# Two output matmuls at a time: regrouping the second layer's blocks in a slot of TensorE's order

## Chip, cores and metric

One NeuronCore of a Trainium2 chip runs the whole program. The metric is the device time of one execution in microseconds (us); lower is better. TensorE (PE in the profile) does matmuls and transposes into PSUM, VectorE (DVE), ScalarE (ACT) and GpSimd (POOL) do elementwise work, and SyncE (SP) issues nearly all DMA transfers.

## What is computed

The input is x, 32 images of 128 channels by 56 by 56 pixels, in float32. Cut to what matters:

```
z = x + relu(batchnorm(conv3x3(sign(ln_channels(x)), sign(w) * alpha) + b))
t = tokens(z)                         # 32 x 3136 tokens x 128 channels
u = layernorm(t)
weights = u @ wr + br                 # one number a token
sel = the 1567 tokens of an image with the largest weights
f[sel] = (gelu(u[sel] @ w1 + b1) @ w2 + b2) * weights[sel];  f = 0 elsewhere
out = from_tokens(t + f + u)
```

w1 is 128 x 512 and w2 512 x 128. The kernel computes the two layers for all tokens and multiplies with a gate that is 0 for the tokens not chosen.

## The kernel before

**Tiling.** Channels lie on the 128 partitions. An image is 3136 columns, worked in 7 chunks of 448 (`NCH = 7`, `T = 448`). Everything below names a chunk by its number c, 0 to 6.

**Two phases.** Phase 1 (up to about 565 us) does the convolution of all images and sums up the batch statistics. Phase 2 does the rest, and the change lies in it alone. It is a software pipeline over images: while image n is in its two layers, image n+1 is normalised, image n+2 gets its residual, and the outcome of image n-1 is gated and stored.

**Positions.** Phase 2 gives each image 56 positions (`POS = 2 * NB * NCH`), in 7 slots of 8. Each engine walks through the same positions, in an order written out by hand, and does at each what tables name for it. `due(table, shift, n, b, pos)` says which steps fall on this position; an entry of 56 or more falls into the next image's positions. In slot c of image n TensorE does:

- positions 0 to 3 of the slot: `hidden`, the four blocks of the first layer of chunk c (three fp16 matmuls each, L939 to L941);
- positions 4 to 7: `output`, the four blocks of the second layer of chunk c-1, accumulated in one PSUM bank (one float32 matmul each; the profile shows each as two MATMUL records of L950). In slot 0 it is the last chunk of the image before. The last block raises `y_done`, and ScalarE copies the bank out (L505) at the eighth position.

**Steps between them.** Behind the hidden or output block of a position TensorE does what the tables place there. In this text each has a short name with its chunk or round:

- T0 to T6 (`TRANSPOSE_AT`, L885): four transposes of a chunk of image n+1 for its layernorm. VectorE takes statistics of each (L647). T2 waits until the statistics of T0 are taken, T3 for those of T1, since they share PSUM banks.
- N0 to N6 (`NORM_AT`, L917 and L920): the statistics as rows of 3 partitions spread to 128 partitions by two matmuls. VectorE scales and centres with them (L685, then L694 one position later), and later forms the base of the output (L702).
- R0 to R6 (`ROUTER_AT`, L895): router weights. After R6 they go through DRAM for the search of the threshold.
- C0 to C7 (`COUNT_AT`, L959): one round each of that search. VectorE counts (L722), TensorE sums the counts (C), VectorE chooses and sets the next candidates (L728, L733, L739) and counts again for the next round.
- G0 to G6 (`OUT_AT`, L930): the gates of image n-1 spread from 3 partitions to 128. VectorE multiplies with them (L781), GpSimd adds the base.
- ST (L904), the mask step (L965 to L967) and the scan (L972), once an image.

The steps that fall on the fifth to eighth position of each slot, behind the output block there, are:

| slot | fifth | sixth | seventh | eighth |
|---|---|---|---|---|
| 0 | T2 | T3, C7 | | N4 |
| 1 | | scan | | R0, N5 |
| 2 | R3, N6 | R4 | | R5, ST |
| 3 | | G2 | | N0 |
| 4 | | | G4 | C1, N1 |
| 5 | | G5 | C3 | N2 |
| 6 | G6 | C5 | N3 | |

VectorE's own order at a position is: choose (L728), first count or gates, tile statistics (L647), L685, L733, L694, L781, L739, L702, next count (L722). L694 of chunk 3 falls on the last position of the image and is VectorE's last instruction there.

**The loop.** `pairs` writes images -1 to 2 and 29 to 32 out straight, and runs images 3 to 28 in a loop on each engine, two images a turn: 13 turns, 12 jumps back to the loop's start (ahead of images 5, 7, ... 27). The loop's own instructions have line L269.

Of the kernel before, what the change touches and what calls it, by code (L numbers as in the profile page):

```python
# [21 lines left out]
NCH = TOK // T  # L22
# [6 lines left out]
NB = HID // C  # L29
# [48 lines left out]
def block_kernel(nc, consts, x_in, cw_in, cb_in, gamma_in, beta_in, wr_in, br_in, w1_in, b1_in,  # L78
# [12 lines left out]
    with ExitStack() as ctx:  # L91
# [167 lines left out]
        def wait_count(eng, semaphore, value):  # L259

            if not (isinstance(value, int) and value <= 0):
                eng.wait_ge(semaphore, value)
# [12 lines left out]
        def is_int(n):  # L275
            return isinstance(n, int)

        def has(n, low=0, high=n_img):

            return not is_int(n) or low <= n < high  # L280
# [6 lines left out]
        def due(table, shift, n, b, pos):  # L287

            steps = [table] if is_int(table) else table
            found = []  # L290
            for at, m, mb in ((pos, n + shift, (b + shift) % 2), (pos + POS, n + shift - 1, (b + shift + 1) % 2)):
                if at in steps and has(m):
                    found.append((m, mb, steps.index(at)))
            return found
# [533 lines left out]
        def _(pe):  # L828
# [46 lines left out]
            def transposes(m, b, c, n, pos):  # L875
                pe.wait_ge(x1_ready, m * NCH + c + 1)

                wait_count(pe, t_ready if c % 2 else u_ready, done(NORM_AT, 1, n, pos))
                if c % 2:
                    wait_count(pe, gated, done(OUT_AT, -1, n, pos))  # L880
                if c > 1:
                    pe.wait_ge(stats_taken, m * NCH + c - 1)
                for i in range(TPG):
                    lo = c * T + i * TILE
                    last = nc.tensor.transpose(ps[0:TILE, BC0 + c % 2, i * C:(i + 1) * C], xb[b][:, lo:lo + TILE], ident)  # L885
                last.then_inc(transposed, 1)

            def router(n, b, c):

                pe.wait_ge(tl_ready, n * NCH + c + 1)  # L890
                if c == 0 and has(n - 1):
                    pe.wait_ge(mask_step, (n - 1) * MASK_STEPS + 3)
                bank = ps[:, T_BANK, 0:T]
                for i, (w, t) in enumerate(((wsel_h, th), (wsel_h, tl), (wsel_l, th))):
                    last = M(bank, w[:, C - c:2 * C - c], cut(t, c), start=c == 0 and i == 0,  # L895
                             stop=c == NCH - 1 and i == 2)
                if c == NCH - 1:
                    last.then_inc(w_done, 1)

            def rows_of_stats(m, n, pos):  # L900
                pe.wait_ge(mr_ready, m + 1)
                wait_count(pe, u_ready, done(NORM_AT, 1, n, pos))
                for q in range(2):
                    last = nc.tensor.transpose(ps[0:NT, BC0, q * C:q * C + TILE], rm[:, q, :],  # L904
                                               ident[0:TILE, 0:TILE])
                last.then_inc(stat_rows, 1)

            def spread_stats(m, b, c, n, pos):

                g = m * NCH + c  # L910
                if c == 0:
                    pe.wait_ge(norm_rows_in, (m + 1) * 2 * PIECES * 16)

                wait_count(pe, u_ready, g)
                wait_count(pe, stats_taken, done(TRANSPOSE_AT, 1, n, pos + 1))
                wait_count(pe, rms_ready, done(STAT_AT, 1, n, pos + 1))
                M(ps[:, BC0, 0:T], ones_b[0:PIECES, :], cut(rows[0:PIECES, :], c), start=True, stop=True).then_inc(bc_stats, 1)  # L917
                wait_count(pe, t_ready, g)
                wait_count(pe, gated, done(OUT_AT, -1, n, pos + 1))
                M(ps[:, BC1, 0:T], ones_b[32:32 + PIECES, :], cut(rows[32:32 + PIECES, :], c), start=True, stop=True).then_inc(bc_stats, 1)  # L920

            def spread_gates(m, b, c, n, pos):
                g = m * NCH + c
                if c == 0:
                    pe.wait_ge(gate_rows_in, (m + 1) * PIECES * 16)

                wait_count(pe, gated, g)
                wait_count(pe, t_ready, done(NORM_AT, 1, n, pos))
                wait_count(pe, stats_taken, done(TRANSPOSE_AT, 1, n, pos + 1))
                M(ps[:, BC1, 0:T], ones_b[64:64 + PIECES, :], cut(rows[64:64 + PIECES, :], c), start=True, stop=True).then_inc(bc_gate, 1)  # L930

            def hidden(n, b, c, j):
                g = n * NCH + c
                if j == 0:
                    pe.wait_ge(tl_ready, g + 1)
                wait_count(pe, h_ready, (g - 1) * NB + j + 1)
                bank = ps[:, H_BANK + j, 0:T]
                blk = slice(j * C, (j + 1) * C)
                M(bank, w1_h[:, blk], cut(th, c), start=True, stop=False)  # L939
                M(bank, w1_h[:, blk], cut(tl, c), start=False, stop=False)  # L940
                M(bank, w1_l[:, blk], cut(th, c), start=False, stop=True).then_inc(h_done, 1)  # L941

            def output(n, b, c, j):
                g = n * NCH + c
                if j == 0:
                    wait_count(pe, y_taken, g)
                first, final = j == 0, j == NB - 1
                bank = ps[:, Y_BANK, 0:T]
                pe.wait_ge(h_ready, g * NB + j + 1)
                last = M(bank, w2_c[:, j, :], hs[(b + c) % 2][:, j, :], start=first, stop=final)  # L950
                if j == NB - 1:
                    last.then_inc(y_done, 1)

            def sum_counts(n, r):

                pe.wait_ge(part_counts, n * ROUNDS + r + 1)
                if r == 0:
                    pe.wait_ge(w_taken, n + 1)
                M(cnt_ps, cnt_c[:, :].to_broadcast([C, C]), cand_sel[:, :], start=True,  # L959
                  stop=True).then_inc(counts_summed, 1)  # L960

            def transpose_ties(n):
                pe.wait_ge(ties_ready, n + 1)
                R = slice(0, MR_ROWS)
                nc.tensor.transpose(ps[0:MR_COLS, T_BANK, 0:MR_ROWS], ties_sb, ident[R, R])  # L965
                M(off_ps, kt[R, K_ONES:K_ONES + MR_ROWS], rowg_c[R, :], start=True, stop=False)
                M(off_ps, kt[R, K_STRI:K_STRI + MR_ROWS], rowe_c[R, :], start=False, stop=True).then_inc(ties_t, 1)  # L967

            def scan_ties(n):

                pe.wait_ge(ties_copied, n + 1)
                M(ps[0:MR_ROWS, T_BANK, C:C + MR_COLS], et[:, :], kt[0:MR_COLS, K_TRIU:K_TRIU + MR_COLS],  # L972
                  start=True, stop=True).then_inc(ties_scanned, 1)

            def phase2(n, b):
                for pos in range(POS):
                    c, j = divmod(pos, 2 * NB)

                    if j < NB and has(n):
                        hidden(n, b, c, j)  # L980
                    if j >= NB and c > 0 and has(n):
                        output(n, b, c - 1, j - NB)
                    if j >= NB and c == 0 and has(n - 1):
                        output(n - 1, 1 - b, NCH - 1, j - NB)

                    at = (n, b, pos)
                    for m, mb, c in due(TRANSPOSE_AT, 1, *at):
                        transposes(m, mb, c, n, pos)
                    for m, mb, c in due(ROUTER_AT, 0, *at):
                        router(m, mb, c)  # L990
                    for m, mb, r in due(COUNT_AT, 0, *at):
                        sum_counts(m, r)
                    for m, mb, _ in due(MASK_AT, 0, *at):
                        transpose_ties(m)
                    for m, mb, _ in due(SCAN_AT, 0, *at):
                        scan_ties(m)
                    for m, mb, _ in due(STAT_AT, 1, *at):
                        rows_of_stats(m, n, pos)
                    for m, mb, c in due(OUT_AT, -1, *at):
                        spread_gates(m, mb, c, n, pos)  # L1000
                    for m, mb, c in due(NORM_AT, 1, *at):
                        spread_stats(m, mb, c, n, pos)

            pairs(pe, phase2, *P2, -1, n_img + 1)


# [20 lines left out]
```

## Time and profile before

| | |
|---|---|
| median of 3 runs | 2377.53 us (2375.41 to 2380.52) |
| time of the profiled execution | 2379.78 us |
| its span, first to last instruction | 2377.8 us |
| busy: PE, DVE, ACT, POOL | 93%, 68%, 51%, 39% |
| mean granted TensorE clock | 0.981 of full |

The profiled execution's own time lies 2.0 us over its span, and 2.3 us over the median of the runs. Busy time is a share of the span; matmuls are pipelined and overlap each other, so that the distance from start to start says more than the time of one. The timeline merges instructions of one line that follow each other ("x4" is four records) and gives the idle time of the engine ahead of an instruction in brackets, with what ended it.

### The profile page before, as it was taken

Reading aid. Unit: us, or ns where it says so; the run is one execution under the profiler, and the core shown is the slowest. Engines: PE = TensorE matmul, PEld = TensorE weight load, DVE = VectorE, ACT = ScalarE, POOL = GpSimd, SP = SyncE. Lnnn points to the kernel's source line nnn. Section 1 sums busy time; section 2 is a strip of 40 time slices with the busy share of each in tenths; the row PEclk is TensorE's granted clock in tenths of the full one; section 3 lists DMA queues with packets and bytes.
Section 4 is the critical chain, followed back from the end, with each engine's and each line's share of the span. In section 5 each row is a group of like instructions: output and inputs, shape, how many; then the busy total and the mean of one; then the engine's idle time right before and its main releaser. Section 6 shows DMA issues by size and latency. Waiting matters only on the chain. (4 is left out here: it accounts for less than half of the span.)

```text
span 2377.8 us, 38759 instructions
## 1 busy us (share of the span) xinstructions
PE 2202.0 (93%) x9739; PEld 1071.6 (45%) x9739; DVE 1622.5 (68%) x4887; ACT 1222.9 (51%) x2030; POOL 918.5 (39%) x714
## 2 busy tenths in 40 slices
PE   6999999966999999999999999998999999999997
PEld 3555555533444444444444444444444444444443
DVE  6777777755677766767676666666667676767764
ACT  4444444434555555555555555555555555555553
POOL 1000000024455544445445555454544454554433
PEclk9999999987999999999999999999999999999998
DMA  3444444431122222222222222222222222222201
GB/s 146 163 162 162 162 162 162 162 122 46 62 73 73 74 81 76 81 85 75 73 73 73 73 73 72 73 73 73 81 82 91 73 73 73 73 73 84 73 33 59
DMA packets 66710, 216.99 MB, mean 91 GB/s; under 512 B 28496, under 2 KB 33328, under 8 KB 62640
## 3 DMA queue, kind: packets, MB, share of 16 engines
q1 hardware_dynamic: 66464, 215.71, 25.1%
q14 instruction: 84, 0.69, 0.1%
q8 instruction: 18, 0.29, 0.1%
q10 hardware_dynamic: 144, 0.30, 0.0%
HBM read 136.70 MB, written 77.47 MB: 90 GB/s over the span
## 5 line engine op out<-in xcount | busy, mean ns | idle before, releaser
L950 PE MATMUL ps<-hs,w_c 128*128 128x448 f32 x1792 | 806.9, 564 | 0.8 <-ACT yo L505 0.6
L495 ACT ACTIVATE hs<-ps,b1c,undo 128x448 f32<-128x448 f32 x896 | 602.6, 718 | 136.6 <-PE ps L941 136.0
L412 POOL TENSOR_TENSOR tl<-tr,th 128x448 f16<-128x448 f32 x224 | 245.5, 1096 | 515.7 <-ACT th L518 393.9
L854 PE MATMUL ps<-yo,cwT 128*128 128x448 bf16 x2016 | 425.6, 356 | 0.0
L950 PEld LDWEIGHTS ps<-hs,w_c 128*128 128x128 f32 x1792 | 305.3, 192 | 191.7 <-issue 152.3
L505 ACT ACTIVATE yo<-ps,cols 128x448 f32<-128x448 f32 x224 | 141.9, 633 | 453.6 <-PE ps L950 453.6
L407 POOL TENSOR_TENSOR xb<-xb,zr 128x448 f32<-128x448 f32 x224 | 259.1, 1159 | 182.7 <-ACT zr L511 181.8
L419 POOL TENSOR_TENSOR yo<-yo,base 128x448 f32<-128x448 f32 x224 | 264.5, 1181 | 167.4 <-DVE yo L781 166.6
L939 PE MATMUL ps<-th,w_h 128*128 128x448 f16 x896 | 321.4, 359 | 0.0
L941 PE MATMUL ps<-th,w_l 128*128 128x448 f16 x896 | 319.3, 356 | 0.0
L940 PE MATMUL ps<-tl,w_h 128*128 128x448 f16 x896 | 319.2, 356 | 0.0
L854 PEld LDWEIGHTS ps<-yo,cwT 128*128 128x128 bf16 x2016 | 179.2, 98 | 196.2 <-issue 48.7
L476 ACT ACTIVATE y<-ps 128x448 f16<-128x448 f32 x224 | 121.9, 544 | 263.2 <-PE ps L854 263.2
L781 DVE TENSOR_TENSOR yo<-yo,ps 128x448 f32<-128x448 f32 x224 | 138.6, 619 | 152.4 <-PE ps L930 150.7
L647 DVE BATCH_NORM_STATS2 st<-ps 112x6 f32<-112x128 f32 x896 | 192.7, 282 | 62.9 <-PE ps L885 60.5
L511 ACT ACTIVATE zr<-y,bn_t,bn_s 128x448 f32<-128x448 f16 x224 | 168.8, 754 | 122.2 <-DMA y<-y_int 109.6
L685 DVE TENSOR_TENSOR ur<-xb,ps 128x448 f32<-128x448 f32 x224 | 138.5, 618 | 134.8 <-PE ps L917 76.5
L571 DVE BATCH_NORM_STATS2 base<-y 128x448 f16 (+1 forms) x224 | 140.5, 627 | 130.2 <-ACT y L476 130.2
L518 ACT ACTIVATE th<-tr 128x448 f16<-128x448 f32 x224 | 129.3, 577 | 139.8 <-DVE tr L694 127.6
L426 POOL TENSOR_TENSOR rm<-stw,kt 112x28 f32<-112x28 f32 x32 | 153.6, 4799 | 78.8 <-DVE stw L665 78.8
L885 PE MATMUL ps<-kt,xb 128*112 128x128 f32 x896 | 140.4, 281 | 41.7 <-DVE st L647 28.8
L403 POOL TENSOR_TENSOR sm<-sm,kt 128x1 f32<-128x1 f32 x1 | 0.6, 566 | 459.7 <-DVE sm L635 459.7
(131 smaller groups left out, 2709.7 us busy)
## 6 DMA issues: line engine op xcount, KB each, us to landing
xb<-x SPq DMA_DIRECT2D x31, 1568.0 KB, 7.6
xb<-x SPq DMA_DIRECT2D x33, 896.0 KB, 4.7
result<-yo SPq DMA_DIRECT2D x32, 896.0 KB, 4.4
y_int<-y SPq DMA_DIRECT2D x32, 784.0 KB, 3.7
xb<-x SPq DMA_DIRECT2D x33, 672.0 KB, 4.3
result<-yo SPq DMA_DIRECT2D x32, 672.0 KB, 3.4
y<-y_int SPq DMA_DIRECT2D x32, 448.0 KB, 5.3
y<-y_int SPq DMA_DIRECT2D x32, 336.0 KB, 4.8
```

The source lines that it names most:

```text
L407: nc.gpsimd.tensor_tensor(cut(xb[b], c), cut(xb[b], c), zr[(b + c) % 2][:, :], ALU.add).then_inc(x1_ready, 1)
L412: nc.gpsimd.tensor_tensor(cut(tl, c), tr[(b + c) % 2][:, :], cut(th, c), ALU.subtract).then_inc(tl_ready, 1)
L419: nc.gpsimd.tensor_tensor(cut(yo[b], c), cut(yo[b], c), cut(base[b], c), ALU.add).then_inc(out_ready, 1)
L426: nc.gpsimd.tensor_tensor(rm[:, 0, :], stw[:, 5, :], kt[0:TILE, K_MHALF:K_END], ALU.pow).then_inc(rstd_ready, 1)
L495: nc.scalar.activation(hs[(b + slot) % 2][:, j, :], ps[:, H_BANK + j, 0:T], ACT.Gelu_apprx_tanh, bias=b1c[:, j:j + 1], scale=undo[:, 1:2]) ...
L511: nc.scalar.activation(zr[(mb + c) % 2][:, :], cut(y16[mb], c), ACT.Relu, bias=bn_t[:, :], scale=bn_s[:, :]).then_inc(relu_ready, 1)
L647: last = V.bn_stats(st[:, c * TPG + i, :], ps[0:TILE, BC0 + c % 2, i * C:(i + 1) * C])
L854: last = M(bank, cwT[:, t, :], sg[b][:, c * ROWS + dy:c * ROWS + dy + ROWS, dx:dx + SIDE], start=t == 0, stop=t == TAPS - 1)
L939: M(bank, w1_h[:, blk], cut(th, c), start=True, stop=False)
L940: M(bank, w1_h[:, blk], cut(tl, c), start=False, stop=False)
L941: M(bank, w1_l[:, blk], cut(th, c), start=False, stop=True).then_inc(h_done, 1)
L950: last = M(bank, w2_c[:, j, :], hs[(b + c) % 2][:, j, :], start=first, stop=final)
```

## The change

The four output blocks of a chunk no longer take one position each. Blocks 0 and 1 are issued at the fifth position of a slot and blocks 2 and 3 at the seventh; the sixth and the eighth issue none. All other steps keep their position and stay behind the output blocks of it. The same instructions are issued, in another order, and only on TensorE.

```diff
                     if j < NB and has(n):
                         hidden(n, b, c, j)
-                    if j >= NB and c > 0 and has(n):
-                        output(n, b, c - 1, j - NB)
-                    if j >= NB and c == 0 and has(n - 1):
-                        output(n - 1, 1 - b, NCH - 1, j - NB)
+                    for k in range(j - NB, j - NB + 2) if j in (NB, NB + 2) else ():
+                        if c > 0 and has(n):
+                            output(n, b, c - 1, k)
+                        if c == 0 and has(n - 1):
+                            output(n - 1, 1 - b, NCH - 1, k)
```

## Rows read from the trace of the kernel before

**Rows 1.** Waits of PE, longest first: in total, times, longest.

```profile
PE ps L917 <- DMA rows<-rms: 43.1, 32, 7.9
PE ps L885 <- DVE st L647: 28.8, 25, 1.3
PE ps L959 <- DVE junk L722: 24.1, 24, 1.3
```

**Rows 2.** Timeline of PE, slot 2: start us, us, instruction.

```profile
1596.23 1.67 PE L950 MATMUL ps<-hs,w_c 128*128 128x448 f32 x4
1597.73 0.35 PE L895 MATMUL ps<-th,wsel_h 128*128 128x448 f16 x1
```

**Rows 3.** Timeline of PE, slot 6, from G6 to the next image.

```profile
1624.86 0.36 PE L930 MATMUL ps<-rows,ones_b 3*128 3x448 bf16 x1
1625.15 1.02 PE L950 MATMUL ps<-hs,w_c 128*128 128x448 f32 x2
...
1626.03 1.00 PE L950 MATMUL ps<-hs,w_c 128*128 128x448 f32 x2
1626.96 0.36 PE L917 MATMUL ps<-rows,ones_b 3*128 3x448 bf16 x1
...
1628.11 0.35 PE L939 MATMUL ps<-th,w_h 128*128 128x448 f16 x1
```

**Rows 4.** Timeline of PE, slots 4 and 5: G4, C1 and C2.

```profile
1613.62 0.36 PE L930 MATMUL ps<-rows,ones_b 3*128 3x448 bf16 x1
...
1614.76 0.17 PE L959 MATMUL ps<-cand_sel,cnt_c 128*128 128x15 f16 x1
...
1617.04 0.18 PE L959 MATMUL ps<-cand_sel,cnt_c 128*128 128x15 f16 x1
```

**Rows 5.** Timeline of DVE over the same stretch.

```profile
1614.01 0.62 DVE L781 TENSOR_TENSOR yo<-yo,ps 128x448 f32<-128x448 f32 x1 [0.85 <-PE ps L930]
1614.99 0.17 DVE L728 TENSOR_SCALAR_CACHE_REDUCE reached<-ps 128x15 f32<-128x15 f32 x1 [0.36 <-PE ps L959]
...
1615.26 0.62 DVE L685 TENSOR_TENSOR ur<-xb,ps 128x448 f32<-128x448 f32 x1
...
1616.35 0.62 DVE L722 TENSOR_SCALAR_CACHE_REDUCE junk<-wse,srch 128x392 bf16<-128x392 f32 x1
```

**Rows 6.** Timeline of DVE, slot 6 and over the loop's jump.

```profile
1625.26 0.62 DVE L781 TENSOR_TENSOR yo<-yo,ps 128x448 f32<-128x448 f32 x1 [0.20 <-PE ps L930]
1625.79 0.62 DVE L702 SCALAR_TENSOR_TENSOR base<-tr,xb 128x448 f32<-128x448 f32 x1
...
1627.64 0.62 DVE L685 TENSOR_TENSOR ur<-xb,ps 128x448 f32<-128x448 f32 x1
1628.35 0.62 DVE L694 TENSOR_TENSOR tr<-ur,ps 128x448 f32<-128x448 f32 x1
1632.24 0.89 DVE L647 BATCH_NORM_STATS2 st<-ps 112x6 f32<-112x128 f32 x4 [3.27 <-PE ps L885]
```

**Rows 7.** Line L269 from 1620 to 1645 us: duration ns, start us.

```profile
L269 DVEq COMPARE_BRANCH  x1: 72/72/72, 1628.5 to 1628.5; - x1
...
L269 DVEq FUSED_REGOPS  x1: 85/85/85, 1632.1 to 1632.1; - x1
```

**Rows 8.** Timeline of PE behind a jump: T2 and T3.

```profile
1633.28 0.62 PE L885 MATMUL ps<-kt,xb 128*112 128x128 f32 x4 [1.09 <-DVE st L647]
...
1635.92 0.62 PE L885 MATMUL ps<-kt,xb 128*112 128x128 f32 x4 [1.26 <-DVE st L647]
```

**Rows 9.** Timeline of DVE between the two images of a turn.

```profile
1686.55 0.62 DVE L694 TENSOR_TENSOR tr<-ur,ps 128x448 f32<-128x448 f32 x1 [0.45 <-issue]
1687.73 0.89 DVE L647 BATCH_NORM_STATS2 st<-ps 112x6 f32<-112x128 f32 x4 [0.56 <-PE ps L885]
```

**Rows 10.** Windows from T3 to N4 behind a jump, instructions of L950 alone.

```profile
core 0: us, PE busy (x) PEld busy (x), PEclk, DMA share, GB/s
...
1521.58:1525.31 3.73, 2.79 (x4) 1.22 (x4) 0.57 0.87 338
1635.92:1638.08 2.16, 1.68 (x4) 0.68 (x4) 1.00 0.87 327
```

## The prediction

> **What bounds the kernel now.** I read the busy shares first, then PE's waits, then the timelines of PE and DVE over one turn of the loop. PE works nearly without a pause in phase 2. What it waits for, in quantity, is three things in an image [rows 1]: N0 waits for rows that come by DMA (32 times), C0 for the first count of VectorE (24 times), and T2 and T3 for VectorE's tile statistics. The first two hang on a fixed delay behind a step of PE itself (ST, R6): whatever PE gains ahead of those steps passes through them, and the change touches nothing between them. The third occurs behind the loop's jumps. There VectorE issues its last L694, branches at once, and its sequencer carries on only 3.6 us later [rows 7]; the statistics of T0 start 3.27 us after L694 has ended [rows 6], and PE stands 1.09 and 1.26 us [rows 8]. So an image has a PE-bound part, and behind each of 12 jumps a point that VectorE sets. The question about each moved step is which of the two it feeds.
>
> **What the change moves.** Steps at the fifth position now come behind output block 1, those at the seventh behind block 3; steps at the sixth and eighth keep their neighbours before them. By the table of steps, four places matter: R3 and N6 in slot 2, G4 in slot 4, C3 in slot 5, and G6 with N3 in slot 6. (T2 only swaps with a block; T3, which follows, waits for VectorE either way.) Output blocks come earlier, so ScalarE's copy isn't held up.
>
> *What PE gains.* Four passes of L950 take 1.50 us, 0.375 each, a block 0.75 [rows 2]. Behind a 3-partition matmul the same block takes longer. From G6 to the next image's L939 is 3.25 us before [rows 3]: G6 0.29, block 1 with C5 0.88, block 2 0.93, N3 1.15 with block 3. I price the parts against the plain 0.75 and 0.19: entering a 3-partition matmul costs 0.09 to 0.10, leaving it 0.10, and a further 0.10 if a float32 block follows it; C costs 0.03, and 0.08 more if a float32 block follows. In the new order of slot 6 (block 1, G6, C5, blocks 2 and 3, N3, then fp16) two such costs go: from block 1's place (1624.77) G6 comes at 1625.61, C5 at 1625.90, block 2 at 1625.92, N3 at 1627.61, L939 at 1627.90 instead of 1628.11. Saved: 0.2 an image. N6 in slot 2, G4 in slot 4 and C3 in slot 5 save 0.10 each, by the same parts. Had PE nothing to wait for, that would be 0.5 an image. No row shows C directly behind G; I take 0.29 for G as before a full matmul, and at worst the whole 0.36 of its record, 0.07 more.
>
> Against a rule: the Trainium skill ("TensorE: Matmul & The Clock Gate", "Step-by-step: what each phase is for") has TensorE pull the next weight load ahead of the running matmul, so regrouping would save nothing and the sum below would come out 7 us worse. The dearer neighbours in the rows of slot 6 say otherwise, so I go by them.
>
> *What VectorE loses, slot 4.* C2 already waits for VectorE. Its chain is C1, choose (L728), L685, L733, count (L722) 1616.35, C2 1617.04 [rows 4, 5]. G4 now comes one block later, 1614.37 instead of 1613.62, so L781 starts at 1614.76 instead of 1614.01. The next full instruction starts 0.53 behind such a one [rows 6], so L728 comes at 1615.30 and not at 1614.99, although C1 itself is a little earlier. L685 follows after 0.10 at the least (it no longer waits for N1), or after the 0.27 of before: 1615.40 to 1615.57, against 1615.26. I take the lower, since N1 is long done: C2 comes 0.14 later (0.31 at most), and the 0.10 that PE saved with G4 is spent in waiting.
>
> *Slot 5.* C3 and N2 keep VectorE busy later, but nothing there waits; PE saves its 0.10.
>
> *Slot 6.* G6 is 0.75 later, and so is L781. From it VectorE runs through L702, L728, L733, L739 and L722 to L685 without an idle mark, 2.38 us [rows 6]. N3, 0.65 later, is there in time (L685 can follow a 3-partition matmul by 0.40 and would be free at 1628.01, VectorE comes at 1628.39). So L685 and L694 are 0.75 later. Together with +0.14 and -0.10: +0.79 us for VectorE's last instruction of an image, while PE's next image starts 0.15 earlier (+0.14 - 0.10 - 0.19).
>
> **The sum, by what follows the image.**
> - Behind a jump (12 times) the branch comes right after L694, so the 3.6 us start 0.79 later, and T3 with them: 12 x 0.79 = +9.5.
> - Between the two images of a turn (13 times) VectorE stood idle 0.56 for T0 [rows 9], and back to back the two would start 0.07 before the end: 0.63 is free, so 0.79 - 0.63 = 0.16 remains: +2.1.
> - In the images written out straight (6 times) L694 has more room, and PE sets the pace: 6 x -0.15 = -0.9.
> - Slot 2 saves 0.10 in all 32: -3.1. N6 makes VectorE 0.75 late there, ahead of ST; ST's input is ready before it by about as much, and if it weren't, up to 0.1 of the gain would go.
>
> That is +7.6 us without the clock.
>
> The Trainium skill ("Runtime: NRT & Kernel Launch", "Instruction fetch mechanics") says that a taken branch whose target lies outside the engine's small instruction memory has to fetch by DMA before it continues. The trace agrees, with VectorE's 3.6 us; by that rule the delay starts at the branch, as summed above, and would not be covered by anything earlier.
>
> *The clock.* Behind 12 jumps the stretch T3 to N4 took 2.16 or 2.17 us at full clock nine times, and 3.64 to 3.75 us at a granted 0.57 to 0.59 three times (a part of it at the lower level, 1.2 GHz) [rows 10]. PE had stood 1.09 and 1.26 us before, with T2 and a block between. Now: PE reaches block 0 0.15 earlier, ends block 1 at 1632.63, T2 comes at 1634.07, ends 1634.51, T3 at 1636.71. That is 1.44 and 2.20 us, 3.6 idle of 4.1, with four short transposes between. If 2.35 us idle let the clock fall in three of twelve, 3.6 with less work between should in all or nearly all. Such a fall cost 1.5 us where it hit the work squarely; if it starts while PE still stands, less. I take 1.3, bounds 0.8 and 1.6. Nine more: +11.7 (7 to 14).
>
> Total +19.3. Against the profiled execution's 2379.8 that is 2399; against the median of the runs (2.3 lower) 2397.
>
> **Rivals.**
> - *VectorE late, clock as before.* The falls stay at about three, since they depend on more than the pause. +7.6, 2385. Against it: the idle time grows by half and is hardly broken.
> - *Faster: the lateness is hidden.* If VectorE's chain from L781 to L694 had 0.79 of room, PE would keep 0.5 an image, 16 us: 2362. It decides where L722 and L685 could start before they do now; the unbroken chain [rows 6] and the wait of C2 speak against it, the fact that between two images 0.63 is free speaks for it.
> - *No change.* The 3.6 us at the jump run from something that isn't moved (a fetch begun earlier), so the jump costs nothing more: 0 + 2.1 - 0.9 - 3.1 = -2, and with no more falls of the clock 2376. Against it: VectorE's branch is stamped right behind L694's start [rows 6, 7], and L694 can't start before L685 has ended, so nothing at the jump can begin before the work that is late.
> - *Worse than forecast.* C2 at +0.31 in all images (5 us more) or second falls of the clock elsewhere: 2408 to 2415.
>
> **How the numbers follow.** Chances: forecast 0.64, clock as before 0.15, faster 0.08, no change 0.06, worse 0.07. 0.2% of the time is 4.8 us, about what a measurement of this kernel can tell from none. The forecast's own range, from 7.6 + 7 with the lower clock bound and 0.07 less or more at the joints: 2391 to 2403. To hold 8 in 10 it takes in the case without clock falls below and the beginning of the worse above: 2382 to 2407. Slower is all but the second and third rival: 0.85; faster 0.08, same 0.07.
>
> **What would show it.** Right: L781 of G6 some 0.75 later against block 0 of slot 6; VectorE's branch about 0.8 later against C0; the two waits at T2 and T3 near 1.4 and 2.2 us; granted clock below 1 from T3 to N4 behind most jumps; C2 waiting near 0.4 us. Wrong: waits at T3 no longer than 1.3 us, a block behind G or N as dear as before, or full clock behind the jumps.

## The result, and the profile after

The changed kernel takes 2411.89 us (median, 2408.0 to 2413.5), the kernel before 2377.92 us in the same comparison: ratio 1.014, 95% interval 1.0123 to 1.0158, 34 us slower. The profiled execution's span is 2411.1 us instead of 2377.8. The forecast had the sign and the mechanism behind the jumps; its 2397 is 15 us short, and the time lies outside its range of 2382 to 2407.

PE's waits in the changed kernel, to be read beside [rows 1] (in total, times, longest):

```profile
PE ps L885 <- DVE st L647: 47.3, 42, 2.0
PE ps L917 <- DMA rows<-rms: 45.9, 32, 7.9
PE ps L959 <- DVE junk L722: 26.7, 27, 1.3
...
PE ps L920 <- DVE yo L781: 10.8, 30, 0.4
```

The waits for tile statistics grew from 28.8 to 47.3 us, as forecast. The last line is new and stands in no step of the forecast: N's second matmul (L920) waits for the gate multiplication (L781), 30 times.

It is in slot 4. The timeline of PE there, to be read beside [rows 4]:

```profile
1749.86 0.36 PE L930 MATMUL ps<-rows,ones_b 3*128 3x448 bf16 x1
1750.15 0.18 PE L959 MATMUL ps<-cand_sel,cnt_c 128*128 128x15 f16 x1
1750.27 0.36 PE L917 MATMUL ps<-rows,ones_b 3*128 3x448 bf16 x1
1751.03 0.34 PE L920 MATMUL ps<-rows,ones_b 3*128 3x448 bf16 x1 [0.40 <-DVE yo L781]
...
1753.02 0.17 PE L959 MATMUL ps<-cand_sel,cnt_c 128*128 128x15 f16 x1
```

and of DVE, beside [rows 5]:

```profile
1750.26 0.62 DVE L781 TENSOR_TENSOR yo<-yo,ps 128x448 f32<-128x448 f32 x1 [1.58 <-PE ps L930]
1750.80 0.17 DVE L728 TENSOR_SCALAR_CACHE_REDUCE reached<-ps 128x15 f32<-128x15 f32 x1
...
1750.89 0.62 DVE L685 TENSOR_TENSOR ur<-xb,ps 128x448 f32<-128x448 f32 x1
...
1751.97 0.62 DVE L722 TENSOR_SCALAR_CACHE_REDUCE junk<-wse,srch 128x392 bf16<-128x392 f32 x1
```

VectorE does what was forecast: L781, L728 0.54 later, L685 right behind, L722 ended at 1752.59. But C2 comes at 1753.02, 0.43 after that. It no longer waits for the count (before, it stood 0.17 us for it); PE's own order makes it late. Both the gate and the second of N's two matmuls write PSUM bank 7 (`BC1`), and the code of N says so:

```python
wait_count(pe, t_ready, g)
wait_count(pe, gated, done(OUT_AT, -1, n, pos + 1))
M(ps[:, BC1, 0:T], ones_b[32:32 + PIECES, :], cut(rows[32:32 + PIECES, :], c), ...
```

Before, block 3 (0.75 us) ran between G4 and N1 and covered the multiplication. Now G4, C1 and N1 follow each other, and L920 starts 0.76 us behind L917 instead of at once. The profile calls 0.40 us of that a wait; over the 30 times it is 0.36 us on the mean.

Slot 6 and the jump. PE, beside [rows 3] and [rows 8]:

```profile
1761.40 0.36 PE L930 MATMUL ps<-rows,ones_b 3*128 3x448 bf16 x1
...
1763.42 0.36 PE L917 MATMUL ps<-rows,ones_b 3*128 3x448 bf16 x1
...
1763.71 0.36 PE L939 MATMUL ps<-th,w_h 128*128 128x448 f16 x1
...
1769.83 0.62 PE L885 MATMUL ps<-kt,xb 128*112 128x128 f32 x4 [1.22 <-DVE st L647]
1772.46 1.07 PE L885 MATMUL ps<-kt,xb 128*112 128x128 f32 x4 [2.01 <-DVE st L647]
```

DVE, beside [rows 6]:

```profile
1761.80 0.62 DVE L781 TENSOR_TENSOR yo<-yo,ps 128x448 f32<-128x448 f32 x1 [0.50 <-PE ps L930]
...
1764.19 0.62 DVE L685 TENSOR_TENSOR ur<-xb,ps 128x448 f32<-128x448 f32 x1
1764.90 0.62 DVE L694 TENSOR_TENSOR tr<-ur,ps 128x448 f32<-128x448 f32 x1
1768.79 0.89 DVE L647 BATCH_NORM_STATS2 st<-ps 112x6 f32<-112x128 f32 x4 [3.28 <-issue]
```

L781 to L685 is 2.39 us (2.38 before), the pause behind L694 3.28 (3.27). The image's first L939 comes 2.31 behind G6 instead of 3.25 (block 1, 0.75 us, now lies ahead of G6, and 0.19 are saved), L694 starts 1.19 behind it instead of 0.24, and the waits at T2 and T3 are 1.22 and 2.01 us.

The windows from T3 to N4 behind the 12 jumps, L950 alone, beside [rows 10] (the fields are those of its first line). Ten of the twelve are below full clock, before it was three; the first, the fourth and the ninth:

```profile
841.91:844.08 2.17, 1.68 (x4) 0.68 (x4) 1.00 0.85 304
...
1189.08:1193.29 4.21, 3.27 (x4) 1.22 (x4) 0.50 0.86 301
...
1772.46:1776.16 3.70, 2.76 (x4) 1.22 (x4) 0.58 0.92 336
```

**Where the 34 us are.** I cut each image at the same instructions in both traces and summed the differences over images 1 to 30, and sorted the forecast's terms (counted for all 32 images) in the same way. The two spans differ by 33.3 us.

| stretch of an image | forecast us | measured us |
|---|---|---|
| C0 to C2 (slot 4) | +4.5 | +16.5 |
| C2 to the next image's first L939 (slots 5, 6) | -9.3 | -11.8 |
| first L939 to T3 | +15.3 | +19.6 |
| T3 to G0 (clock) | +11.7 | +10.3 |
| G0 to R6 (slot 2) | -3.1 | -2.7 |
| R6 to C0 (N0) | 0 | +3.1 |
| sum | +19.1 | +35.0 |

The first row alone is 12 of the 16 us that are missing, but not all of it is one thing. In most images C0 to C2 is 0.40 or 0.48 us longer, 13.3 us in 30 images at the median of 0.44; the other 3 are TensorE's clock, which fell in this stretch in six images of the changed kernel (granted clock 0.79 to 0.94 there) and in four of the kernel before (0.90 to 0.93).

### The profile page after: what moved, and what is told of

Same layout as the page of the kernel before. It is cut to its first block and busy times, and to the rows that moved or that the text cites. A ratio compares the mean times of both kernels' runs of the same rounds, so it can differ in the third digit from the quotient of the medians.

```text
span 2411.1 us, 38759 instructions
## 1 busy us (share of the span) xinstructions
PE 2204.2 (91%) x9739; PEld 1086.5 (45%) x9739; DVE 1632.3 (68%) x4887; ACT 1220.2 (51%) x2030; POOL 918.0 (38%) x714
## 5 line engine op out<-in xcount | busy, mean ns | idle before, releaser
L950 PE MATMUL ps<-hs,w_c 128*128 128x448 f32 x1792 | 781.1, 563 | 0.2 <-ACT yo L505 0.2
L412 POOL TENSOR_TENSOR tl<-tr,th 128x448 f16<-128x448 f32 x224 | 242.5, 1083 | 551.5 <-ACT th L518 459.5
L950 PEld LDWEIGHTS ps<-hs,w_c 128*128 128x128 f32 x1792 | 326.0, 195 | 221.1 <-issue 196.5
L407 POOL TENSOR_TENSOR xb<-xb,zr 128x448 f32<-128x448 f32 x224 | 258.3, 1155 | 186.3 <-ACT zr L511 185.5
L419 POOL TENSOR_TENSOR yo<-yo,base 128x448 f32<-128x448 f32 x224 | 266.6, 1190 | 160.9 <-DVE yo L781 160.0
L939 PE MATMUL ps<-th,w_h 128*128 128x448 f16 x896 | 320.8, 358 | 0.0
L781 DVE TENSOR_TENSOR yo<-yo,ps 128x448 f32<-128x448 f32 x224 | 138.5, 618 | 193.1 <-PE ps L930 193.1
L685 DVE TENSOR_TENSOR ur<-xb,ps 128x448 f32<-128x448 f32 x224 | 138.5, 618 | 165.9 <-PE ps L920 86.7
L885 PE MATMUL ps<-kt,xb 128*112 128x128 f32 x896 | 141.6, 283 | 60.5 <-DVE st L647 47.3
L426 POOL TENSOR_TENSOR rm<-stw,kt 112x28 f32<-112x28 f32 x32 | 153.5, 4797 | 78.6 <-DVE stw L665 78.6
```

Of the source, the lines that this page charges most:

```text
L407: nc.gpsimd.tensor_tensor(cut(xb[b], c), cut(xb[b], c), zr[(b + c) % 2][:, :], ALU.add).then_inc(x1_ready, 1)
L412: nc.gpsimd.tensor_tensor(cut(tl, c), tr[(b + c) % 2][:, :], cut(th, c), ALU.subtract).then_inc(tl_ready, 1)
L419: nc.gpsimd.tensor_tensor(cut(yo[b], c), cut(yo[b], c), cut(base[b], c), ALU.add).then_inc(out_ready, 1)
L426: nc.gpsimd.tensor_tensor(rm[:, 0, :], stw[:, 5, :], kt[0:TILE, K_MHALF:K_END], ALU.pow).then_inc(rstd_ready, 1)
```

## The experiments

Times are medians; each was compared with the kernel before on its own chip, which took 2376.4 to 2378.1 there. "Over before" is the ratio with its 95% interval. Differences in the text are between medians; the interval of a ratio reaches 2 to 5 us to either side. Lines of kernel.py below the place of an edit that adds lines have higher numbers in that run's views: L920 is L921 and L885 is L886 where VectorE is written out straight, and L885, L917 and L950 are L888, L920 and L953 with the extra matmuls.

| kernel | us | over before |
|---|---|---|
| the change | 2411.9 | 1.0140 (1.0123 to 1.0158) |
| slot4_alone | 2388.1 | 1.0036 (1.0022 to 1.0050) |
| slot6_alone | 2412.9 | 1.0143 (1.0129 to 1.0157) |
| slots_2_and_5 | 2376.2 | 0.9992 (0.9983 to 1.0001) |
| all_but_slot4 | 2399.9 | 1.0101 (1.0085 to 1.0116) |
| after_n1_later | 2395.5 | 1.0069 (1.0054 to 1.0085) |
| before_n1_later | 2369.4 | 0.9967 (0.9955 to 0.9979) |
| after_filled | 2399.0 | 1.0091 (1.0078 to 1.0104) |
| after_straight | 2355.4 | 0.9906 (0.9891 to 0.9922) |
| before_straight | 2339.6 | 0.9853 (0.9837 to 0.9869) |
| before_straight_n1 | 2335.9 | 0.9836 (0.9817 to 0.9855) |
| after_straight_n1 | 2333.9 | 0.9824 (0.9810 to 0.9837) |
| before_straight_n1_s5 | 2333.0 | 0.9819 (0.9806 to 0.9833) |

### Slot by slot

```diff
-                    for k in range(j - NB, j - NB + 2) if j in (NB, NB + 2) else ():
+                    if c in SLOTS:
+                        blocks = range(j - NB, j - NB + 2) if j in (NB, NB + 2) else ()
+                    else:
+                        blocks = (j - NB,) if j >= NB else ()
+                    for k in blocks:
```

SLOTS stands for what each run has in its place: (4,), (6,), (2, 5) and (0, 1, 2, 3, 5, 6).

**Slot 4 alone.** 

> The kernel before with the output blocks paired in slot 4 alone, so that G4 alone comes later. Theory A (bank): N1's second matmul writes the PSUM bank that G4 filled and waits in TensorE's order until VectorE has multiplied with it; TensorE stands 0.3 to 0.4 us there, C0 to C2 grows by 0.48, and since little of it is given back the time grows by 10 to 15 us. Theory B (VectorE's queue alone, as forecast): C2 comes 0.14 later, the time grows by 3 to 5 us, and the second matmul of N1 follows the first without a wait.

The new line of the waits is there unchanged (L920 for L781: 10.8 us, 30 times), with no other slot changed, and C0 to C2 is 0.40 or 0.48 us longer in most images (16.1 us in 30 images, falls of the clock among them). The total is +10.0 us (by the ratio's interval 5 to 12), and +11.9 over the 30 images of the traces: 3.0 us come back between C2 and C3, the 0.10 that G4's place saves, and one fall of the clock behind a jump fewer is in this trace. Theory A had the place and the size of the wait; the time lies at the lower end of its 10 to 15 us, and above theory B's 3 to 5.

**Slot 6 alone.** 

> The kernel before with the output blocks paired in slot 6 alone, so that G6 and N3 alone come later. Theory A (VectorE's last instruction of an image sets T3 behind a jump): branch and T3 later by 0.75 us behind the 12 jumps, by 0.2 to 0.3 between the images of a turn, more falls of the clock behind the jumps: +15 to +22 us. Rival (TensorE sets the pace; the saved 0.19 us an image counts): -6 us, no more clock falls than before.

Worse than theory A: +34.9 us, as much as the whole change. In the trace the image's first L939 to T3 adds 19.5 us, as in the changed kernel, and PE saves 5.8 us in slot 6. The rest is clock. Behind all 12 jumps it is low, and the windows T3 to N4 are longer than in the changed kernel; here the first and the ninth, the only one of the twelve under 4.20:

```profile
837.95:842.16 4.21, 3.27 (x4) 1.23 (x4) 0.50 0.78 303
...
1773.47:1776.11 2.64, 1.71 (x4) 0.75 (x4) 0.81 0.84 320
```

T3 to G0 adds 19.3 us and C0 to C1 another 6.1, all of it at the lower clock. So the parts don't add up: slots 4 and 6 give 45 us one by one, the whole change 34. One difference stands in the trace. Here slot 0 has its old order, with one block ahead of T2 and one between T2 and T3, and the stall is long first and short after it:

```profile
1885.98 0.62 PE L885 MATMUL ps<-kt,xb 128*112 128x128 f32 x4 [1.95 <-DVE st L647]
1886.44 1.05 PE L950 MATMUL ps<-hs,w_c 128*128 128x448 f32 x2
1888.61 1.07 PE L885 MATMUL ps<-kt,xb 128*112 128x128 f32 x4 [1.12 <-DVE st L647]
```

In the changed kernel slot 0 is paired too, both blocks lie ahead of T2, and the waits are 1.22 and 2.01 us: nearly the same standing in all, another order, and shorter falls. all_but_slot4, with the same waits as the changed kernel, adds 8.1 us from T3 to G0 where slot6_alone adds 19.3. That slot 0's order makes this difference was not tried alone.

**Slots 2 and 5.** 

> The kernel before with pairs in slots 2 and 5 alone. Theory A (the entry and exit of a 3-partition matmul and of a count between float32 blocks cost TensorE 0.1 us each, and these two slots feed nothing that VectorE makes late): 0.2 us saved in each of 32 images, -4 to -6 us. Rival (later N6, C3 and N2 cost as much at the next wait, or the saving is lost at the waits of N0, C0 and T3): within 2 us of before.

The rival: -1.8 us, and the interval holds 1. In the trace slot 2 saves 2.7 us and slot 5 2.3, near their price, and they are lost again: 2.8 us between R6 and C0, where N0 comes 0.1 us later, and 1.9 at T2 behind the jumps, where T2 comes 0.16 later against the image's start. N0 hangs on ST's chain of VectorE, and there one step has become longer: the third of its four (L678) takes 502 ns on the mean in the changed kernel and 506 here, 416 before, the others 378 or 379 as before. L670 ahead of them went from 563 to 853 (857 here). GpSimd's work lies elsewhere beside them than before. Over all 32 images L670 takes 0.18 us where no GpSimd instruction runs beside it (one case before, two after), 0.58 on the mean beside L407 (30 cases before) and 0.89 beside L419 (29 cases after); L678 takes 0.26 or 0.27 alone and 0.37 to 0.69 beside L407. Others don't change: L685 takes 0.61 or 0.62 us beside GpSimd and alone. L670 reads two tensors in SBUF, L685 one there and one in PSUM. So far the traces show what goes together; no run moved GpSimd's work alone.

**All but slot 4.** 

> The changed kernel with slot 4 put back to one block a position. Theory A (bank wait of N1 in slot 4): C0 to C2 back to 5.95 us, 10 to 15 us faster than the changed kernel, so +19 to +24 over before, near the forecast +19. Theory B (slot 4 costs only 0.14 us): 3 to 5 us faster than the changed kernel.

12 us faster than the changed kernel, and C0 to C2 as before (0.0 us difference in most of the 30 images, -0.1 in the sum): theory A. And +22 over before is within 3 us of the forecast's +19.3, which was made with next to nothing for slot 4. That it comes so near is in part luck: two terms that the forecast hadn't (4 us from the image's start to T3, 3 at N0) stand against a smaller one for the clock (8.1 instead of 11.7).

### N1 one position later

```diff
-NORM_AT = [31, 39, 47, 54, 63, 71, 76]
+NORM_AT = [31, 40, 47, 54, 63, 71, 76]
```

> The changed kernel with N1 at position 40 instead of 39, behind the first hidden block of slot 5 (L694, L518 and L412 of that chunk move one position with it). Theory A (N1's second matmul waits for the gate multiply because both use one PSUM bank): one hidden block of 0.57 us runs while VectorE multiplies, the wait of 0.3 to 0.4 us shrinks to nearly nothing, C0 to C2 is about 0.3 us shorter, 8 to 12 us faster than the changed kernel. Theory B (VectorE's queue ahead of C2): C2 waits for the count as before, less than 3 us gained.

> Control: the kernel before with the same N1 at position 40. There N1 doesn't wait for the bank, so by theory A nothing is gained; L685 moves behind the count on VectorE, so C2 may stop waiting 0.17 us: between 0 and -5 us against before.

The changed kernel gains 16.4 us by it (8 to 12 were expected), the kernel before 8.6. The line of L920 is gone from the waits, and PE runs through; G4, C1 and the hidden block lie in front of N1:

```profile
1739.22 0.35 PE L941 MATMUL ps<-th,w_l 128*128 128x448 f16 x1
1739.50 0.36 PE L917 MATMUL ps<-rows,ones_b 3*128 3x448 bf16 x1
1739.68 0.34 PE L920 MATMUL ps<-rows,ones_b 3*128 3x448 bf16 x1
...
1741.10 0.17 PE L959 MATMUL ps<-cand_sel,cnt_c 128*128 128x15 f16 x1
```

Between the traces C0 to C2 is 0.57 us shorter in the changed kernel and 0.15 in the kernel before (at the median of the images), where no bank wait existed and only VectorE's order (L685 behind the count) helps. The difference, 0.42 us, is 12.6 us in 30 images, nearly the whole 13.3 by which the changed order makes C2 late. That shows theory A. The total times give less for it, 7.8 us (16.4 less 8.6); falls of the clock and the spread of the runs are in that number too. The second expectation was too cautious: 8.6 us instead of at most 5. In its trace 0.15 an image make 4.5 us, but the sum from C0 to C2 is only 2.1, since falls of the clock there cost more than in the kernel before; behind the jumps there is one fall fewer. The profiled execution took 4.4 us more than the median, so the trace doesn't show where all of the 8.6 comes from, and that stays open.

### The clock

Seven matmuls of 384 columns ahead of T2's transposes, in every second image:

```diff
+                if c == 2 and b == 0:
+                    for _ in range(7):
+                        M(ps[:, BC0, 0:3 * C], cwT[:, 0, :], cwT[:, 1:4, :].rearrange("p t c -> p (t c)"), start=True, stop=True)
```

> The changed kernel with seven extra bf16 matmuls of 384 columns ahead of T2's transposes in every second image, those that follow a jump among them (their result is overwritten at once by the transposes, so the output is the same). They take 1.1 us of TensorE's time while it would stand for T3. Theory A (the clock falls behind the jumps because TensorE stands too long there): T3 at the same place, granted clock 1.0 from T3 to N4 behind most jumps instead of 2 of 12, 8 to 12 us faster than the changed kernel. Rival (the falls have another cause, or the cost of a fall is given back at the wait of G0): no faster, or slower by the extra work.

Theory A: 12.9 us faster than the changed kernel with more work on TensorE. All 12 windows from T3 to N4 are at full clock. PE's timeline and one window of it:

```profile
1759.38 1.30 PE L885 MATMUL ps<-cwT 128*128 128x384 bf16 x7 [1.22 <-DVE st L647]
1760.51 0.60 PE L888 MATMUL ps<-kt,xb 128*112 128x128 f32 x4
1762.00 0.62 PE L888 MATMUL ps<-kt,xb 128*112 128x128 f32 x4 [0.89 <-DVE st L647]
```

```profile
1762.00:1764.17 2.17, 1.68 (x4) 0.68 (x4) 1.00 0.88 304
```

The wait of 1.22 us is that of the changed kernel; the 2.01 at T3 has become 1.1 us of throwaway work and 0.89 of waiting, and behind the jumps T3 isn't later for it (it is 0.6 to 0.8 us later in three images that follow no jump). The falls behind the jumps come from TensorE's standing there. Ten of them cost some 13 us, 1.3 each, which is the price that the forecast took.

### The jump

VectorE's part of phase 2 without the loop:

```diff
-            pairs(dve, phase2, *P2, -1, n_img + 1)
+            for n in range(-1, n_img + 1):
+                phase2(n, n % 2)
```

> The changed kernel with VectorE's part of phase 2 written out straight, no loop and no jump on VectorE; the other engines keep their loops. Theory A (VectorE's jump of 3.6 us turns its lateness into TensorE's wait): the 12 waits at T2 and T3 shrink to those of the other images, 12 x 2.9 = 35 us and the clock falls with them, 10 to 14 us: -40 to -50 us, 2362 to 2372. Rival (the 3.6 us come from something other than the jump, such as fetching the next instructions, which straight code needs as well): less than 10 us gained.

> The kernel before with VectorE's part of phase 2 written out straight (control for the same edit on the changed kernel, which took 2355). Theory A (the 3.6 us of VectorE's jump are all that is special behind a jump): T3 comes 2.48 us earlier behind each of 12 jumps and the three clock falls there go: 12 x 2.48 + 3 x 1.3 = 34 us, 2344, so that the change still costs 10 to 14 us without any jump, from slot 4 and from VectorE's lateness at T3. Rival (the change costs only through the jump): 2353 to 2357, the same as the changed kernel with straight VectorE.

The changed kernel gains 56 us, more than the 40 to 50 expected, and the kernel before 37. The sum of T2 and T3's waits in the changed kernel goes from 47.3 us to 8.1:

```profile
PE ps L921 <- DVE yo L781: 10.8, 30, 0.4
PE ps L905 <- DVE rm L670: 8.5, 1, 8.5
PE ps L886 <- DVE st L647: 8.1, 30, 0.6
```

So the 3.6 us are the jump's, and straight code of many more instructions doesn't have them. The change still costs 15.8 us without VectorE's jump (expected 10 to 14). The line of the bank wait stands at 10.8 us as before, and the next section shows that with it nearly all of the 15.8 goes.

### Both, and what is left of the change

> The kernel before with VectorE straight and N1 at position 40: the two edits touch different waits (T3 behind a jump, C2), so they add: 34 us and 4 to 8 us, 2336 to 2340. Rival (the time saved at C2 is lost again at T3, where VectorE then sets the pace): no faster than with straight VectorE alone.

> As before_straight_n1, with the output blocks of slot 5 alone paired, the one slot whose moved step (C3) feeds nothing that is late: 0.10 us in each of 32 images, -3 us against it. Rival: within 1 us of it.

> The changed kernel with VectorE straight and N1 at position 40: with the jump and the bank wait gone, what is left of the change is 0.5 us an image saved by TensorE against VectorE's lateness at T3 (0.1 to 0.2) and the rest at N0 (0.1) and C2 (0.1). Theory A: within 4 us of before_straight_n1, in either direction. Rival (more is wrong with the order than these two waits): 8 us or more slower than before_straight_n1.

With the jump and the bank wait gone the changed order takes 2333.9 us and the order before 2335.9. The intervals overlap, so no difference can be told, and the rival, that more is wrong with the order, falls. In the changed order N1's move is worth 21.5 us (2355.4 to 2333.9), in the order before 3.8. The 0.10 us of slot 5, alone on top, gives 2333.0, -2.9 as expected but inside the intervals. It has the lowest median here, 1.8% under the kernel before; nearly all of that is the jump (1.5%).

## Why the prediction was wrong

By its own steps:

- **What bounds the kernel.** Right. PE-bound stretches, and a point behind each jump that VectorE sets; without the jump (before_straight) the kernel gains 37 us.
- **What PE gains.** Right: 0.11, 0.10 and 0.19 us an image in slots 2, 5 and 6 (at the median), where 0.10, 0.10 and 0.2 were forecast. The rule that regrouping saves nothing, against which the forecast went, doesn't hold in these places.
- **What VectorE loses, slot 4: the step that failed.** It says that L685 "no longer waits for N1", "since N1 is long done", and prices C2 at +0.14, at most +0.31. VectorE's chain was right to 0.1 us. The failure is on PE: the forecast moved G4 next to N1 and didn't ask whether N1 may start. It may not, because N1's second matmul takes the bank that VectorE still reads for G4. TensorE stands 0.36 us on the mean, C2 comes 0.40 to 0.48 later against C0 and no longer waits for VectorE. The forecast had 0.14. The price is 12.6 us by the traces of after_n1_later and before_n1_later; by total times it is 7.8 us from these two, 10.0 from slot4_alone, 12.0 from all_but_slot4 and 17.7 from the pairs with straight VectorE, for a step that the forecast put at 4.5. No row of before shows this wait, since block 3 covered it entirely; only the code line names it.
- **Slot 6 and the jump.** Right: L781 to L685 2.39 us, the pause 3.28 us, T3 0.94 us later against the image's start behind a jump (forecast 0.94). The forecast says that the trace agrees with a fetch at the branch; it agrees in VectorE's 3.6 us, but TensorE's jump of the same turn took 0.27 us from its branch to the loop's first instruction. No run here tells what the 3.6 us are spent on.
- **Between images of a turn, and the straight ones.** Forecast 0.31 and 0 later against the image's start, measured about 0.5 and 0.25 to 0.35. Between images of a turn VectorE arrives as forecast (in the straight ones 0.13 later), but from its first tile statistics to T3 it takes 3.78 us instead of 3.55; L702 in between takes 0.84 instead of 0.62. About 4 us. In the changed kernel it overlaps L412 of GpSimd by 0.36 us, in the kernel before L412 had ended:

```profile
1687.86 1.04 POOL L412 TENSOR_TENSOR tl<-tr,th 128x448 f16<-128x448 f32 x1 [2.62 <-ACT th L518]
1689.18 0.61 DVE L702 SCALAR_TENSOR_TENSOR base<-tr,xb 128x448 f32<-128x448 f32 x1
```

```profile
1826.57 1.04 POOL L412 TENSOR_TENSOR tl<-tr,th 128x448 f16<-128x448 f32 x1 [2.62 <-ACT th L518]
1827.24 0.85 DVE L702 SCALAR_TENSOR_TENSOR base<-tr,xb 128x448 f32<-128x448 f32 x1
```

In images 5 to 30 of both traces this L702 takes 0.83 to 0.85 us wherever it overlaps L412 and 0.61 to 0.63 wherever it doesn't.

- **Slot 2.** The saving is there and N0 gives it back (3 us), which the forecast excluded by "ST's input is ready before it": it was, but the chain behind ST got longer.
- **The clock.** Forecast nine more falls of 1.3 us. Measured seven more, 1.2 to 1.4 us each by G0, and one of the three old ones 1.5 longer: 10.3 us instead of 11.7. By after_filled the ten cost 12.9. Right; the certainty about "all or nearly all" was a little too great. The step from 2.35 to 3.6 us idle is too long, though: the first is counted to the end of a record, the second from start to start. Counted like the first, the changed kernel stands 3.23 us (1.22 and 2.01); T2 to T3 is 2.63 us from start to start, where 2.64 was forecast.
- **The rivals.** "Worse than forecast" had the direction, and its 2408 to 2415 holds the measured time, with 0.31 at C2 and falls of the clock elsewhere. C2 was 0.44 later, by another mechanism than the one it names; some falls elsewhere did come (3 us between C0 and C2). Its 0.07 was too little for the one term that rested on an assumption about a wait that no row shows. "Clock as before", "faster" and "no change" fell: the falls are shown, slot6_alone is 35 us slower, and in the changed kernel's trace the pause of 3.28 us stands behind an L694 that comes 0.95 later against the image's start, and T3 comes later with it.

## What to carry to other kernels

When a step is moved next to another, look up in the code which buffer each writes and who still reads it; the trace of before shows no row for a wait that was covered by exactly the block that is moved away. Work that an in-order engine does last before a jump back in its loop is on the critical path if the engine pays for the jump, and a stall there can be paid twice, the second time in TensorE's clock. Where the clock falls, the parts of such a change don't add up in time, so compare them in the trace, stretch by stretch.

## What the runs showed of the hardware

From VectorE's branch to the first instruction of its loop 3.64 to 3.68 us pass at the 12 jumps of phase 2. At 11 of its 13 jumps of phase 1, whose turn has far fewer instructions (some 80 records on VectorE, against 475), it is 0.29 (0.31 and 0.34 at the other two). TensorE's jumps in phase 2 take 0.27 or 0.28, though its turn has more instructions than VectorE's. In straight code on VectorE the statistics of T0 start 1.77 us behind the image's first L939 in all 30 images; behind a jump it was 4.1 before and 5.1 with the change.

Behind the waits at T2 and T3 TensorE's granted clock was below full in 3 of 12 cases before (waits of 1.09 and 1.26 us), in 10 of 12 in the changed kernel (1.22 and 2.01) and in 12 of 12 in slot6_alone (1.95 and 1.12 in the lines shown), and the stretch T3 to N4 then took 2.64 to 4.21 us instead of 2.17. 1.1 us of throwaway matmuls inside the wait kept the clock at full in 12 of 12 cases.

Some VectorE instructions are longer beside GpSimd's work, in the same form: L670 0.18 us alone and 0.58 or 0.89 on the mean beside it, L702 0.62 and 0.84 beside L412 in the place shown, while L702 stays at 0.62 beside L426 (31 cases) and L685 everywhere. The traces show that the two go together; no run took GpSimd's work away.
